# A two-attention transformer layer in fp32: how the scores and the weighing of the values go through TensorE

## Chip, cores and metric

One core of one Trainium2 chip. The metric is device time in microseconds of one execution. TensorE (PE) multiplies and transposes, VectorE (DVE) and ScalarE (ACT) read its results from PSUM, GpSimd (POOL) works on SBUF alone, SyncE (SP) issues the DMAs.

## The reference

32 sequences of 128 tokens, 512 features, 16 heads of 32. In fp32:

```python
ln_out = layernorm(hidden_states, ln1_s, ln1_b)
q, k, v = jnp.split(ln_out @ w_qkv + b_qkv, 3, axis=-1)
scores = jnp.einsum('bhqd,bhkd->bhqk', q, k) / jnp.sqrt(jnp.float32(HD))
scores = scores * mask - 10000.0 * (1.0 - mask)
probs = jax.nn.softmax(scores, axis=-1)
ctx = jnp.einsum('bhqk,bhkd->bhqd', probs, v)
x = hidden_states + ctx @ w_ao + b_ao
# the same once more, with queries from layernorm(x), keys and values from the encoder states
return x + gelu(layernorm(x) @ w1 + b1) @ w2 + b2
```

## The kernel before, in words

Matrix products take fp32 operands apart into a high and a low part, both of the faster type fp32r, and add up three products (low x high, high x low, high x high). Wherever a matrix is made that TensorE needs later, ScalarE makes the high part (a rounding copy) and VectorE the low part (what is left).

Attention works on groups `g` of two sequences (`b` 0 and 1): groups 0 to 15 self-attention, 16 to 31 cross-attention. A group has eight slots `n`; the loops run over groups, with a body of eight slots. In a slot each engine runs a written-out list of calls (the function `slot` of each engine, L629, L777, L928, L1075, and L436 for the DMA queue), and the order in it is fixed. Engines wait for each other by semaphores only. One slot is four heads (chunk `c`, 128 features) of one sequence: `c, b = divmod(n, 2)`.

What TensorE does for one group: the normalised x is transposed (`flip_x`, four 128x128 transposes; for cross groups the encoder rows too, `flip_enc`). `keys` and `queries` (`columns`, L519: 12 products of 256 columns) fill the bank `ps_c`; ScalarE and VectorE empty it into `k_r` and `q_r` before the next may start. `values` and `outputs` (`rows`, L530: two halves of six products of 512 columns) use the bank `ps_r`. For the scores of a slot, keys are placed block-diagonally in `k_bd` by DMA (`place_k`, four per chunk), so that one product of 512 columns gives four heads: three products (L492). VectorE multiplies by the mask (L837), POOL adds the mask's other part (L1046), VectorE takes the row maximum (L852). ScalarE negates it (L697) and takes four exponentials (L704), not normalised. TensorE transposes the four heads (L502), ScalarE and VectorE make an fp16 high and low part (L688, L843), and TensorE multiplies each with the values in three bf16 parts and a column of ones (`v_b`, L515: eight products of 97 columns). VectorE adds the three parts, inverts the sum and multiplies (L864, L866, L870) to give `ctx_t`, which is transposed when a sequence is complete (`flip_ctx`) and goes to `outputs`.

The softmax runs through the slots with a lag: scores of slot n, maximum and exponentials of n-1, transposes of n-2, values of n-3. Keys and queries of chunk c+1 are made in the slots of chunk c, so that each slot of TensorE has scores, transposes, a product with the values, and one or two of `keys`, `queries`, `values` and `outputs`. Layer norms of the next group (L900 to L926, `root` on POOL) lie between the slots' calls. The MLP follows when attention has ended; it shares only the weights' buffers and `mlp_xT` with it.

Lines that the prediction speaks of: L492 scores, L502 transposes, L515 values, L524 columns, L536 rows, L594 flips, L675 (`bias_products`, the only product of true fp32 operands), L688, L697, L704, L723 on ScalarE, L837, L852, L870, L885, L900, L915, L924 on VectorE, L1046 and L1072 on POOL.

Of the kernel before, what the change touches and what calls it, by code (L numbers as in the profile page):

```python
# [8 lines left out]
F32 = mybir.dt.float32  # L9
# [5 lines left out]
P = 128  # L15
# [5 lines left out]


LIFT = 15.0 * math.log(2.0)
VW = 3 * HD + 1
VPAD = VW + 1
# [33 lines left out]
def xattn_layer(nc, a, out):  # L59
# [22 lines left out]
    with ExitStack() as top:  # L82
# [17 lines left out]
        lift_t = sb("lift_t", [P, 1])  # L100
        s_const = sem("const_ready")
        CONSTANTS = 7
# [25 lines left out]
        k_bd = sb("k_bd", [P, 2, 2, GB, HQ * P], F32R)  # L128

        assert GB * HQ * 2 == KC * MB  # L130
        mlp_xT = k_bd[:].rearrange("p i h b t -> p (i h b t)").rearrange("p (h c t) -> p h c t", h=2, c=KC)
# [16 lines left out]
        def pieces(st, u, chunks=range(KC)):  # L148
# [7 lines left out]
            (-1, 4): pieces(SELF, WK), (-1, 5): pieces(SELF, WQ), (-1, 6): pieces(SELF, WV),  # L156
            (1, 0): pieces(SELF, WO),
            (NG - 1, 3): pieces(CROSS, WV, FRONT), (NG - 1, 4): pieces(CROSS, WK),
            (NG - 1, 5): pieces(CROSS, WQ), (NG - 1, 6): pieces(CROSS, WV, BACK),
            (NG + 1, 0): pieces(CROSS, WO),  # L160
# [71 lines left out]
        kbd_in = [sem(f"kbd_in{i}") for i in range(2)]  # L232
        names = ("sc_done pt_done pv_done k_done q_done v_done o_done xT_done encT_done cT_done exp_done pth_done "
                 "kh_done qh_done v1_done v2_done xTh_done encTh_done cTh_done masked mx_done nb_done ptl_done "
                 "kl_done ql_done vr_done v0_done y_copied xTl_done encTl_done cTl_done stats_done aggr_done "
                 "rstd_done xn_done centred eps_added sums_done ctx_done y_done biased v3_done mask_ready res_ready kbd_clear ones_ready")
        s = {name: sem(name) for name in names.split()}

        def attention(st):

# [20 lines left out]
            q_r = buf("q_r", [P, 2, 2, GB * P], F32R)  # L261
            k_r = buf("k_r", [P, 2, 2, GB * P], F32R)
            v_b = buf("v_b", [P, GB, NH, VPAD], BF16)
            v_rest = buf("v_rest", [P, GB, H])
# [3 lines left out]
            nb = buf("nb", [P, 2, HQ])  # L268
            pT = buf("pT", [P, 2, 2, HQ * P], F16)
            csum = buf("csum", [P, 2, HQ, HD])  # L270
            rcp = buf("rcp", [P, 2, HQ])
            ctx_t = buf("ctx_t", [P, GB, H])
# [19 lines left out]
            def leads(g):  # L292


                return isinstance(g, int) and g >= gN
# [27 lines left out]
            def run(engine, slot):  # L323


                for n in range(4, NS):
                    slot(-1, n, False, False, True)
# [1101 lines left out]
```

## Time and profile before

| what | value |
|---|---|
| device time, median of 3 | 2083.93 us (2080.98 to 2086.44) |
| profiled execution: span from first to last instruction | 2081.6 us |
| busy: PE, DVE, ACT, POOL | 94%, 67%, 52%, 42% |
| attention ends, MLP begins | about 1346 us |
| PE's mean granted clock | 0.993 of full |

The page gives no other time for the profiled execution than its span; it is 2.3 us below the median of the runs. In rows of the order of time, the first number is the start and the second the duration of the run of equal instructions; a bracket is the engine's idle time in front of it and what ended that. Durations overlap: the next instruction of an engine starts before the end of the one in front, so that the distance from start to start is the cost of an instruction in a queue.

### The profile page before, as it was taken

What the parts mean: (1) busy time and instruction counts of PE and PEld (TensorE: products, weight loads), DVE (VectorE), ACT (ScalarE), POOL (GpSimd) and SP (SyncE); (2) the same over time, 40 slices, a digit from 0 to 9 for tenths busy, and PEclk for the clock granted to TensorE, in tenths of its full rate; (3) what the DMA queues carried; (4) which work ended last, traced back from release to release, by engine and by line L of the source; (5) the groups of instructions that cost most, each with busy time, mean ns of one, the idle gap of its engine ahead of it and who ended that gap; (6) DMA issues with size and microseconds to landing.
All of it is one profiled execution on the core that took longest, in us unless ns stands there. A gap on an engine that the chain in (4) does not pass through costs nothing. (4 is left out here: it accounts for less than half of the span.)

```text
span 2081.6 us, 39412 instructions
## 1 busy us (share of the span) xinstructions
PE 1957.9 (94%) x12304; PEld 1657.1 (80%) x12304; DVE 1390.2 (67%) x2571; ACT 1072.6 (52%) x2562; POOL 884.1 (42%) x910
## 2 busy tenths in 40 slices
PE   5999999999998999999999999699999999999999
PEld 5788888888787778887887887588888888888887
DVE  6889889888888998899889888662322323232221
ACT  4666666667667666666676666443222222222222
POOL 5556556556557655555565555450201012020110
PEclk9999999999999999999999999899999999999999
DMA  6332222222223432332232224501010101101010
GB/s 172 94 91 70 65 77 68 66 72 74 61 73 88 106 97 73 86 93 72 77 96 71 73 83 104 165 28 51 11 55 5 60 12 48 50 10 54 6 41 21
DMA packets 144820, 141.51 MB, mean 68 GB/s; under 512 B 20736, under 2 KB 94464, under 8 KB 144768
## 3 DMA queue, kind: packets, MB, share of 16 engines
q1 hardware_dynamic: 144768, 140.85, 24.2%
q8 instruction: 28, 0.46, 0.1%
q14 instruction: 24, 0.20, 0.0%
HBM read 82.07 MB, written 25.17 MB: 52 GB/s over the span
## 5 line engine op out<-in xcount | busy, mean ns | idle before, releaser
L1046 POOL TENSOR_TENSOR a_t_s<-a_t_s,a_m_add 128x512 f32<-128x512 f32 x256 | 345.4, 1349 | 334.3 <-DVE a_t_s L837 334.1
L1315 DVE TENSOR_TENSOR m_g_r<-m_g_t,m_g_r 128x512 fp32r<-128x512 f32 x128 | 95.9, 750 | 476.1 <-ACT m_g_r L1294 476.0
L1223 PE MATMUL m_ps_h<-k_bd,wt 128*128 128x512 f32 x1536 | 378.7, 397 | 2.9 <-PEq L360 2.9
L1223 PEld LDWEIGHTS m_ps_h<-k_bd,wt 128*128 128x128 f32 x1536 | 289.2, 189 | 72.4 <-issue 3.3
L1237 PE MATMUL m_ps_y<-m_down_hi,m_g_r 128*128 128x512 f32 x1024 | 343.8, 396 | 0.1
L704 ACT ACTIVATE a_p_s<-a_t_s,a_nb 128x128 f32<-128x128 f32 x1024 | 328.3, 391 | 8.3
L524 PE MATMUL a_ps_c<-a_xT,wt 128*128 128x256 f32 x2304 | 318.2, 288 | 11.6 <-DVE a_xT L885 5.5
L524 PEld LDWEIGHTS a_ps_c<-a_xT,wt 128*128 128x128 f32 x2304 | 285.4, 191 | 25.3 <-issue 10.9
L1237 PEld LDWEIGHTS m_ps_y<-m_down_hi,m_g_r 128*128 128x128 f32 x1024 | 192.4, 188 | 45.1 <-issue 0.5
L1278 ACT ACTIVATE m_g_t<-m_ps_h,bias_cols 128x512 f32<-128x512 f32 x128 | 88.1, 688 | 270.9 <-PE m_ps_h L1223 270.7
L688 ACT CAST a_pT<-a_ps_t 128x512 f16<-128x512 f32 x256 | 150.0, 586 | 150.7 <-PE a_ps_t L502 150.4
L492 PE MATMUL a_ps_s<-k_bd,a_q_r 128*128 128x512 f32 x768 | 221.7, 397 | 0.0
L536 PE MATMUL a_ps_r<-wt,a_cT 128*128 128x512 f32 x768 | 209.2, 408 | 1.3 <-ACT a_y_t L752 1.3
L1376 POOL TENSOR_TENSOR m_rstd<-m_mv,eps_t 128x1 f32<-128x1 f32 x28 | 5.3, 189 | 478.6 <-DVE m_mv L1331 478.6
L843 DVE TENSOR_TENSOR a_pT<-a_ps_t,a_pT 128x512 f16<-128x512 f32 x256 | 174.3, 681 | 41.1 <-ACT a_pT L688 41.1
L1237 PE MATMUL m_ps_y<-wt,m_g_r 128*128 128x512 f32 x512 | 201.2, 393 | 0.0
L1294 ACT CAST m_g_r<-m_g_t 128x512 fp32r<-128x512 f32 x128 | 79.5, 621 | 236.0 <-PE m_ps_y L1237 234.6
L837 DVE TENSOR_TENSOR a_t_s<-a_ps_s,a_m_mul 128x512 f32<-128x512 f32 x256 | 174.3, 681 | 29.0 <-PE a_ps_s L492 27.8
L852 DVE TENSOR_REDUCE a_mx<-a_t_s 128x4 f32<-128x512 f32 x256 | 172.7, 675 | 2.5
L492 PEld LDWEIGHTS a_ps_s<-k_bd,a_q_r 128*128 128x128 f32 x768 | 140.1, 189 | 29.1 <-issue 1.0
L515 PE MATMUL a_ps_o<-a_v_b,a_pT 128*128 128x97 bf16 x2048 | 133.5, 207 | 29.3 <-POOL a_v_b L1052 14.9
L502 PEld LDWEIGHTS a_ps_t<-ident,a_p_s 128*128 128x128 f32 x1024 | 127.2, 140 | 42.3 <-ACT a_p_s L704 7.3
(85 smaller groups left out, 3210.9 us busy)
## 6 DMA issues: line engine op xcount, KB each, us to landing
k_bd<-a_k_r SPq DMA_DIRECT2D x512, 64.0 KB, 2.1
a_x_t<-in_x SPq DMA_DIRECT2D x32, 256.0 KB, 2.8
a_res_t<-in_x SPq DMA_DIRECT2D x32, 256.0 KB, 2.8
x_after_self<-a_y_t SPq DMA_DIRECT2D x32, 256.0 KB, 2.0
a_x_t<-x_after_self SPq DMA_DIRECT2D x32, 256.0 KB, 2.7
a_enc_t<-in_ctx SPq DMA_DIRECT2D x32, 256.0 KB, 2.9
raw_wt<-in_w SPq DMA_DIRECT2D x32, 256.0 KB, 4.7
a_res_t<-x_after_self SPq DMA_DIRECT2D x32, 256.0 KB, 3.9
```

The costliest lines, as they stand in the source:

```text
L492: last = nc.tensor.matmul(ps_s[n % 2][:], q_r[:, i, hq, b * P:(b + 1) * P], k_bd[:, i, hk, b], start=(x == 0), stop=(x == 2))
L515: last = nc.tensor.matmul(ps_o[:, j, 0:VW], pT[:, n % 2, h, j * P:(j + 1) * P], v_b[:, b, HQ * c + j, 0:VW], start=(h == HI), stop=(h == LO))
L524: last = nc.tensor.matmul(ps_c[:, 0:GB * P], weights(g, hw)[:, unit, kc, c * P:(c + 1) * P], xt[:, hx, kc], start=(k == 0), stop=(k == 3 * ...
L536: last = nc.tensor.matmul(ps_r[:], lhs(hx, kc), weights(g, hw)[:, unit, kc], start=(k == 0), stop=(k == 2 * n - 1))
L688: nc.scalar.copy(pT[:, n % 2, HI], ps_t[n % 2][:].rearrange("p j t -> p (j t)")).then_inc(s["pth_done"], 1)
L704: last = nc.scalar.activation(p_s[:, n % 2, j], t_s[:, n % 2, j], ACT.Exp, bias=nb[:, n % 2, j:j + 1])
L837: nc.vector.tensor_tensor(t_s[:, n % 2], ps_s[n % 2][:], m_mul[:, b].unsqueeze(1).to_broadcast([P, HQ, P]), ALU.mult).then_inc(s["masked"], 1)
L843: nc.vector.tensor_tensor(pT[:, n % 2, LO], ps_t[n % 2][:].rearrange("p j t -> p (j t)"), pT[:, n % 2, HI], ALU.subtract).then_inc(s["ptl_ ...
L852: nc.vector.tensor_reduce(mx[:, n % 2], t_s[:, n % 2], AX_X, ALU.max).then_inc(s["mx_done"], 1)
L1046: nc.gpsimd.tensor_tensor(t_s[:, n % 2], t_s[:, n % 2], m_add[:, b].unsqueeze(1).to_broadcast([P, HQ, P]), ALU.add).then_inc(s["biased"], 1)
L1223: last = nc.tensor.matmul(ps_h[j % 2][:], w1[hw][:, j // KC, kc, (j % KC) * P:(j % KC + 1) * P], xT[:, hx, kc], start=(k == 0), stop=(k == ...
L1237: last = nc.tensor.matmul(ps_y[b][:], g_r[:, j % 2, hg, b * P:(b + 1) * P], w2[hw][:, j // KC, j % KC], start=(j == 0 and x == 0), stop=(j ...
```

## The change

- Keys and queries stay in fp32 (`k_t`, `q_t`), copied out of `ps_c` by ScalarE alone. The scores of a whole sequence are made at once, for each head and chunk one fp32 product over the head's 32 rows, 128 columns; the four heads of a chunk lie in four 32-row strips and four PSUM banks. `k_bd` and its DMAs go.
- The order of heads in slots changes: `b, c = divmod(n, 4)`. All keys and queries of the next group are made in slots 4 to 7, values and outputs in slots 0 to 3.
- The exponentials give their sums too (`accum_out`). VectorE inverts the sums and normalises the probabilities, which TensorE transposes and ScalarE copies once, in fp32. Per head, fp32 values (32 columns) are the stationary operand and the transposed probabilities the moving one, so that the product comes out as a 32-partition strip of the transposed context, in `ps_o`; the context's flip goes.
- `ps_x` goes: flips use `ps_c`. There is one bank for `ps_t` instead of two.
- x is loaded two groups ahead; weight splits, stores and residual loads move to other slots.

```diff
-            ps_s = [ps(f"a_ps_s{i}", [P, HQ, P], F32, st) for i in range(2)]
-            ps_t = [ps(f"a_ps_t{i}", [P, HQ, P], F32, st) for i in range(2)]
-            ps_c = ps("a_ps_c", [P, H], F32, st)
+            ps_s = ps("a_ps_s", [P, HQ, KC, P], F32, st)
+            ps_t = ps("a_ps_t", [P, HQ, P], F32, st)
+            ps_c = ps("a_ps_c", [P, KC, P], F32, st)
             ps_r = ps("a_ps_r", [P, H], F32, st)
-            ps_o = ps("a_ps_o", [P, HQ, P], F32, st)
-            ps_x = ps("a_ps_x", [P, KC, P], F32, st)
+            ps_o = ps("a_ps_o", [P, KC, P], F32, st)
...
+                    def scores(g, b):
+                        pe.wait_ge(s["k_copied"], at((g + 1) * KC))
+                        pe.wait_ge(s["q_copied"], at((g + 1) * KC))
+                        if b > 0 or known(g, 1):
+                            pe.wait_ge(s["masked"], at((g * GB + b) * KC))
+                        cols = slice(b * P, (b + 1) * P)
+                        for c in range(KC):
+                            for j in range(HQ):
+                                r = slice(HD * j, HD * (j + 1))
+                                last = nc.tensor.matmul(ps_s[:, j, c], q_t[r, c, cols], k_t[r, c, cols],
+                                                        start=True, stop=True)
+                        last.then_inc(s["sc_done"], 1)
...
                     def transpose_probs(g, n):
+                        pe.wait_ge(s["normal"], at(slot_no(g, n)))
+                        if n >= 1 or known(g, 1):
+                            pe.wait_ge(s["pT_copied"], at(slot_no(*lag(g, n, 1))))
...
                     def weigh_values(g, n):
+                        b, c = divmod(n, KC)
+                        pe.wait_ge(s["pT_copied"], at(slot_no(g, n)))
...
                         for j in range(HQ):
+                            h = HQ * c + j
+                            last = nc.tensor.matmul(ps_o[HD * j:HD * (j + 1), c], v_t[:, b, HD * h:HD * (h + 1)],
+                                                    pT[:, n % 2, j], start=True, stop=True)
...
                     def keys(g, c):
                         if c > 0 or known(g, 1):
-                            pe.wait_ge(s["ql_done"], at(g * KC + c))
+                            pe.wait_ge(s["q_copied"], at(g * KC + c))
                     def queries(g, c):
-                        pe.wait_ge(s["kl_done"], at(g * KC + c + 1))
+                        pe.wait_ge(s["k_copied"], at(g * KC + c + 1))
...
                     def flip_enc(g, b):
                         pe.wait_ge(enc_in[b], at(16 * (g - NG + 1)))
+                        pe.wait_ge(s["xTl_done"], at(g * GB + b + 1))
                         flip(enc_t, b, "encT_done")
...
                     def slot(g, n, cur, prev, nxt):          # TensorE
+                        if n in (0, 3) and prev:
+                            outputs(g - 1, n // 3, 0, cur)
+                        if n in (1, 2) and cur:
+                            values(g, n - 1, 0)
+                        if n >= 4 and nxt:
+                            keys(g + 1, n - 4)
+                        if n in (0, 1):
+                            if n == 0 and prev:
+                                outputs(g - 1, 0, 1, cur)
+                            if n == 1 and cur:
+                                values(g, 0, 1)
+                        if cur if n >= 3 else prev:
+                            weigh_values(*lag(g, n, 3))
+                        if n == 2 and cur:
+                            values(g, 1, 1)
+                        if n == 3 and prev:
+                            outputs(g - 1, 1, 1, cur)
+                        if n >= 4 and nxt:
+                            queries(g + 1, n - 4)
                         if cur if n >= 2 else prev:
                             transpose_probs(*lag(g, n, 2))
...
+                        if n in (2, 3) and nxt:
+                            flip_x(g + 1, n - 2)
+                            if crosses(g + 1):
+                                flip_enc(g + 1, n - 2)
+                        if n == 3 and cur:
+                            scores(g, 1)
                         if n == 7 and nxt:
+                            scores(g + 1, 0)
...
                     def exponent(g, n):                      # ScalarE
                         act.wait_ge(s["mx_done"], at(slot_no(g, n)))
-                        nc.scalar.activation(nb[:, n % 2], mx[:, n % 2], ACT.Identity, bias=lift_t[:],
-                                             scale=-1.0).then_inc(s["nb_done"], 1)
...
                         for j in range(HQ):
                             last = nc.scalar.activation(p_s[:, n % 2, j], t_s[:, n % 2, j], ACT.Exp,
-                                                        bias=nb[:, n % 2, j:j + 1])
+                                                        bias=mx[:, n % 2, j:j + 1],
+                                                        accum_out=sums[:, n % 2, j:j + 1])
...
+                        if cur if n >= 3 else prev:
+                            copy_probs(*lag(g, n, 3))
                         if cur if n >= 1 else prev:
                             exponent(*lag(g, n, 1))
+                        if n >= 4 and nxt:
+                            copy_cols(g + 1, n - 4, WK, k_t, "k_done", "k_copied")
+                        if n == 2 and prev:
+                            high_context(g - 1, 1)
+                        if n == 6 and cur:
+                            high_context(g, 0)
                         if cur or prev:
                             split_weights(g, n)
+                        if n in (0, 3) and prev:
+                            output_row(g - 1, n // 3)
+                        if n in (1, 2) and cur:
+                            copy_values(g, n - 1)
+                        if n >= 4 and nxt:
+                            copy_cols(g + 1, n - 4, WQ, q_t, "q_done", "q_copied")
...
+                        if n in (2, 3) and nxt:
+                            flip_x(g + 1, n - 2)
...
+                    def invert_sums(g, n):                   # VectorE
+                        dve.wait_ge(s["exp_done"], at(slot_no(g, n)))
+                        nc.vector.reciprocal(rcp[:, n % 2], sums[:, n % 2]).then_inc(s["inverted"], 1)
+                    def normalise(g, n):
+                        dve.wait_ge(s["inverted"], at(slot_no(g, n)))
+                        nc.vector.tensor_tensor(p_s[:, n % 2], p_s[:, n % 2],
+                                                rcp[:, n % 2].unsqueeze(2).to_broadcast([P, HQ, P]),
+                                                ALU.mult).then_inc(s["normal"], 1)
...
+                        if n == 2 and ahead:
+                            norm(g + 1, 1)
                         if cur if n >= 1 else prev:
                             maxima(*lag(g, n, 1))
                         if cur:
                             mask_scores(g, n)
+                        if n == 0 and ahead:
+                            statistics(g + 1, 0)
+                            statistics(g + 1, 1)
                         if cur if n >= 2 else prev:
+                            invert_sums(*lag(g, n, 2))
...
                         if cur if n >= 2 else prev:
+                            normalise(*lag(g, n, 2))
...
+                            moments(g + 1, 0)
+                            moments(g + 1, 1)
+                        if n == 1 and ahead:
+                            centre(g + 1, 0)
+                            norm(g + 1, 0)
+                            centre(g + 1, 1)
+                        if n == 2 and prev:
+                            low_context(g - 1, 1)
+                        if n == 6 and cur:
+                            low_context(g, 0)
...
+                        if n in (2, 3) and nxt:
+                            flip_x(g + 1, n - 2)
+                            if crosses(g + 1):
+                                flip_enc(g + 1, n - 2)
```

## Rows read from the trace of the kernel before

**Rows 1.** The page: busy time, and the span in 40 slices (digits are tenths).
```profile
PE 1957.9 (94%) x12304; PEld 1657.1 (80%) x12304; DVE 1390.2 (67%) x2571; ACT 1072.6 (52%) x2562; POOL 884.1 (42%) x910
...
PE   5999999999998999999999999699999999999999
...
DVE  6889889888888998899889888662322323232221
```

**Rows 2.** Windows: stretch, its length, busy us (instructions) per engine, TensorE's clock, DMA.
```profile
401.30:440.60 39.30, 37.09 (x282) 32.56 (x281) 34.71 (x69) 26.14 (x69) 23.44 (x25) 1.00 0.27 70
...
1004.30:1045.00 40.70, 38.28 (x292) 33.32 (x290) 36.53 (x71) 27.12 (x71) 23.43 (x25) 1.00 0.30 81
1302.00:1346.00 44.00, 27.90 (x168) 22.02 (x166) 30.82 (x56) 19.04 (x46) 21.35 (x19) 0.81 0.46 150
1346.00:2081.00 735.00, 729.38 (x3184) 588.49 (x3184) 219.96 (x314) 198.21 (x313) 99.48 (x102) 1.00 0.10 35
```

**Rows 3.** TensorE's order of time: start, duration, line, tiles, count, idle time before.
```profile
410.36 0.63 PE L594 MATMUL a_ps_x<-ident,a_xn 128*128 128x128 f32 x4 [1.56 <-DVE a_xT L885]
...
415.61 1.64 PE L536 MATMUL a_ps_r<-wt,a_cT 128*128 128x512 f32 x6
417.09 1.53 PE L524 MATMUL a_ps_c<-a_xT,wt 128*128 128x256 f32 x12
418.45 0.86 PE L492 MATMUL a_ps_s<-k_bd,a_q_r 128*128 128x512 f32 x3
419.15 0.60 PE L502 MATMUL a_ps_t<-ident,a_p_s 128*128 128x128 f32 x4
419.59 0.52 PE L515 MATMUL a_ps_o<-a_v_b,a_pT 128*128 128x97 bf16 x8
419.93 1.63 PE L524 MATMUL a_ps_c<-a_xT,wt 128*128 128x256 f32 x12
421.39 1.54 PE L536 MATMUL a_ps_r<-wt,a_xT 128*128 128x512 f32 x6
...
648.94 0.63 PE L594 MATMUL a_ps_x<-ident,a_enc_t 128*128 128x128 f32 x4 [2.28 <-DVE a_encT L885]
```

**Rows 4.** TensorE's order of time where the true fp32 products run.
```profile
64.86 3.60 PE L675 MATMUL a_ps_x<-raw_wt,a_cv 128*128 128x512 f32 x8
```

**Rows 5.** ScalarE's order of time in one slot.
```profile
418.65 0.47 ACT L723 ACTIVATE a_q_r<-a_ps_c,bias_cols 128x256 fp32r<-128x256 f32 x1 [0.94 <-PE a_ps_c L524]
...
419.79 0.58 ACT L688 CAST a_pT<-a_ps_t 128x512 f16<-128x512 f32 x1 [0.19 <-PE a_ps_t L502]
420.27 0.30 ACT L697 ACTIVATE a_nb<-a_mx,lift_t 128x4 f32<-128x4 f32 x1
420.60 1.28 ACT L704 ACTIVATE a_p_s<-a_t_s,a_nb 128x128 f32<-128x128 f32 x4
```

**Rows 6.** VectorE's order of time, four of its instructions.
```profile
402.60 1.58 DVE L915 SCALAR_TENSOR_TENSOR a_xn<-a_x_t,a_mv,norm_row 128x512 f32<-128x512 f32 x1
404.10 0.74 DVE L924 SCALAR_TENSOR_TENSOR a_xn<-a_xn,a_rstd,norm_row 128x512 f32<-128x512 f32 x1
...
407.88 1.35 DVE L870 TENSOR_TENSOR a_ctx_t<-a_csum,a_rcp 128x128 f32<-128x128 f32 x1
...
410.73 0.67 DVE L837 TENSOR_TENSOR a_t_s<-a_ps_s,a_m_mul 128x512 f32<-128x512 f32 x1
```

**Rows 7.** POOL's order of time beside them.
```profile
407.81 1.26 POOL L1072 TENSOR_TENSOR a_res_t<-a_res_t,bias_row 128x512 f32<-128x512 f32 x1
411.48 1.29 POOL L1046 TENSOR_TENSOR a_t_s<-a_t_s,a_m_add 128x512 f32<-128x512 f32 x1 [2.41 <-DVE a_t_s L837]
```

**Rows 8.** TensorE's order of time: the first scores and the last.
```profile
29.88 0.86 PE L492 MATMUL a_ps_s<-k_bd,a_q_r 128*128 128x512 f32 x3
...
1313.27 0.86 PE L492 MATMUL a_ps_s<-k_bd,a_q_r 128*128 128x512 f32 x3
```

**Rows 9.** One line's instructions, 66 to 1300 us: durations in ns, minimum, median, maximum.
```profile
L870 DVE TENSOR_TENSOR a_ctx_t<-a_csum,a_rcp x243: 291/294/1360, 71.5 to 1296.3; 128x128 f32<-128x128 f32 x122
```

More of the change, by code:

```diff
@@ L20 @@
 MASKED = 10000.0
-LIFT = 15.0 * math.log(2.0)
-VW = 3 * HD + 1
-VPAD = VW + 1
 HI, LO = 0, 1
@@ L231, in xattn_layer @@
         stored = [sem(f"stored{b}") for b in range(GB)]
[L232 to L236, printed above, removed]
+        names = ("sc_done pt_done pv_done k_done q_done v_done o_done xT_done encT_done cT_done exp_done pT_copied "
+                 "k_copied q_copied v_copied xTh_done encTh_done cTh_done masked mx_done inverted normal "
+                 "y_copied xTl_done encTl_done cTl_done stats_done aggr_done "
+                 "rstd_done xn_done centred eps_added y_done biased mask_ready res_ready")
         s = {name: sem(name) for name in names.split()}
@@ L323, in run @@
             def run(engine, slot):
-                for n in range(4, NS):
+                for n in range(2, NS):
                     slot(-1, n, False, False, True)
@@ L331, in run @@
                     slot(1, n, True, True, True)
-                with engine.Fori(0, NG - 3) as i:
+                with engine.Fori(0, NG - 4) as i:
                     g = Looped(i, 1, 2)
@@ L342, in run @@
                         slot(g, n, True, True, True)
+                for n in range(NS):
+                    slot(gN - 2, n, True, True, True)
                 for n in range(NS):
@@ L875, in low_cols @@
-                    def low_cols(g, c, unit, dst_t, high, low):
-                        dve.wait_ge(s[high], at(g * KC + c + 1))
-                        i = c % 2
-                        nc.vector.scalar_tensor_tensor(
-                            out=dst_t[:, i, LO], in0=ps_c[:, 0:GB * P],
-                            scalar=bias_cols[:, crosses(g), KC * unit + c:KC * unit + c + 1], in1=dst_t[:, i, HI],
-                            op0=ALU.add, op1=ALU.subtract).then_inc(s[low], 1)
-                    def low_flip(hi_t, lo_t, high, count, low):
+                            dve.wait_ge(s["exp_done"], at(slot_no(*lag(g, n, 2))))
@@ L934, in slot @@
                             mask_scores(g, n)
-                        if n == 4 and ahead:
-                            norm(g + 1, 1)
+                        if n == 0 and ahead:
+                            statistics(g + 1, 0)
+                            statistics(g + 1, 1)
                         if cur if n >= 2 else prev:
-                            low_probs(*lag(g, n, 2))
-                        if n in (1, 2) and ahead:
-                            statistics(g + 1, n - 1)
-                        if n in (2, 3) and prev:
-                            flip_ctx(g - 1, n - 2)
@@ L971, in slot @@
+                        if not (cur or prev) and n >= 4:
+                            split_weights(g, n)
                         if n in (0, 1, 4, 5) and leads(g):
                             flip_x(g + n // 4, n % 4)
-                        if n in (1, 3) and ahead:
-                            centre(g + 1, n // 2)
-                        if n == 3 and ahead:
-                            norm(g + 1, 0)
                     def spread_value_bias(st):
```

415 lines of the change are left out of this document (119 added, 296 removed).

## The prediction, made before the change was run

> **What bounds the kernel now.** The busy table and the slices come first: TensorE is at nine tenths nearly everywhere, VectorE at eight to nine until the 25th slice, then it falls [rows 1]. So there are two stages: attention, 16 self and 16 cross groups of two sequences, until 1346 us [rows 2], then the MLP, 735 us with TensorE 99% busy [rows 2], which the change leaves alone. The windows by stage give one period: 39.3 us for a self group, 40.7 for a cross group, TensorE busy for 37.1 and 38.3 of them [rows 2]. TensorE's order of time shows a slot without waits (417.09 to 421.39 us): columns 1.36 to 1.46, rows 1.48, scores 0.70, transposes 0.44, values 0.34, start to start [rows 3]. TensorE's queue bounds attention, and its one long wait in a self group is the flip of x that waits for the one before it, 1.56 us [rows 3].
>
> **TensorE's work.** A true fp32 call is two instructions: the eight L675 instructions (four calls, 512 columns) take 3.60 us, 0.43 each, against 0.25 for a single-pass one (1.48 by six) [rows 3, 4]. A 128-column fp32 instruction takes 0.11 (transposes, 0.44 by four). Scores become 16 calls, 32 instructions, per sequence. Side by side in no way they cost 32 x 0.108 = 3.45 us; fed as fast as the values of before, eight in 0.34 us, 32 cost 1.36. I take 1.75: a call's two halves use the same 32 rows and run in turn (16 x 0.107), neighbours overlap. Values become 8 instructions per slot, 0.34 to 0.86; by the same argument 0.43. The context's flip (four transposes, 0.44) goes, twice per group. TensorE's sum is then 8 x 1.46 + 8 x 1.48 + 8 x 0.44 + 2 x 0.44 + 2 x 1.75 + 8 x 0.43 = 34.9 us per self group, less than the 37.1 of now: the question is only who makes it wait.
>
> The Trainium skill, "TensorEngine Tiling (Array Packing)", section Theoretical Speedup, gives up to 4x where a dimension is at most 32. By it scores would take 0.86, and the sum below would be some 28 us less. The same page, section Key Properties, says that a change of tiling mode drains the engine; no row here shows a switch, but a drain as long as the tail of the transposes (0.60 busy for 0.44 of pitch) at the four edges of scores would make it some 20 us more.
>
> **Slots 4 to 7: one loop through ScalarE.** There is one bank, ps_c, for the columns. Keys fill it, ScalarE copies it, queries may start (k_copied), ScalarE copies again, the next keys may start (q_copied). ScalarE's own order in the slot is copy_probs, the four exponentials, copy of keys, copy of queries; behind a late exponential stand both copies, and TensorE waits for them. Before, other TensorE work stood between the two fills of ps_c in every slot; now only the short values. The loop [rows 5]: copy_probs 0.49 (0.58 less the overlap of 0.09), exponentials E, key copy 0.46, semaphore 0.05, queries 1.45 plus 0.20 until ScalarE sees the end [rows 3], query copy 0.46 less 0.06: 3.05 + E, near enough. E is 1.19 now. The sums (accum_out) have no row. Free, E stays 1.19, below which it can't fall. As four further instructions like the smallest of ScalarE, L697 with 0.30 [rows 5], without overlap, E is 4 x (0.39 + 0.30) = 2.76. The nearest row is that instruction with the overlap of its neighbours: 4 x (0.30 + 0.21) = 2.04, which I take. Loop: 5.05 us (4.2 to 5.8), where a slot is 4.9 now on the mean.
>
> **Slots 0 to 3: a chain through VectorE.** VectorE loses low_probs, the context's reduction and product and low_cols; it gets a reciprocal (0.2) and normalise. That product is from SBUF, 128x512: 0.66 as L924 (0.74 less an overlap of 0.08), but such instructions wait for POOL: L870 took 1.35 instead of 0.29 beside POOL's 407.81 instruction, and centre (L915) 1.58 instead of 0.74 [rows 6, 7]. POOL starts add_bias 0.08 after the mask ends (411.40, 411.48), 1.29 long, so normalise behind the mask usually stands some 1.2. From the scores' end, VectorE does: slot 0, maximum and mask 1.2, two statistics 1.2 (priced as the mask), reciprocal and normalise 0.9, POOL 0.3, moments 0.2; slot 1, maximum, mask, reciprocal, normalise 2.1, centre, norm, centre 2.0, and 0 to 2.6 for POOL's two additions, of which I take 0.65; slot 2, norm 0.66, maximum and mask 1.2, POOL 1.37, normalise 0.66. With 0.2 to see the scores, the probabilities of slot 0 are normalised at 12.6. TensorE asks for them at 2 x (2.96 + 0.43 + 0.44) + 2.96 + 0.43 = 11.05, and waits. Then a chain: transposes 0.44, flip 0.44, 0.2, ScalarE 0.58, VectorE's low part 0.62, maximum 0.60, mask 0.67, POOL 1.37, normalise 0.70: 5.6, because the low part stands in front of the next maximum in VectorE's order. Then transposes and flip 0.88 and scores 1.75, which cover the wait of keys for the second flip (0.2 + 0.58 + 0.62). Slots 0 to 3: 12.6 + 5.6 + 0.88 + 1.75 = 20.8.
>
> **The sum.** Self group: 20.8 + 4 x 5.05 + 1.75 (scores of slot 7) = 42.75, +3.45. A cross group flips the encoder's rows too, through the same ps_c, directly behind x: twice 0.44 and a wait of 1.45 (0.25, 0.58, 0.62; 2.28 and 1.56 in like places now [rows 3]), 3.8 in all: 46.55, +5.85. The 31 periods but the last, 15.5 of each kind: 15.5 x 9.3 = +144. Edges: all keys and queries of group 0 now come ahead of the first scores (29.9 us now [rows 8]), some +7; the last group has no next columns and flips, and behind its last scores there are fewer steps than in the 33 us of now: together -15 (-30 to +10). The block-diagonal placements on SP's queue go; in the rows above TensorE waits for none of them, so they give nothing. POOL's lost value splits (1.1 each, four per group) shorten no wait but those counted. 2081.6 + 144 - 15 = 2211, and with the 2.3 us by which the median, 2083.9, is above this execution's span: **2213 us**.
>
> **Rivals.** (1) *ScalarE's loop stays as short as today.* Sums cost nothing (E = 1.19), and POOL lets normalise pass in slots 0 and 1 so that TensorE doesn't wait at 11.05. For it: L870's median is 0.29, so most of them met no POOL [rows 9]; before, ScalarE waits long per group for TensorE, busy 26.1 of 39.3 us [rows 2]. Against: POOL now follows the mask directly. Self 11.05 + 5.6 + 0.88 + 1.75 + 4 x 4.24 + 1.75 = 38.0, cross 41.8: 15.5 x (-1.3 + 1.1) - 15 = -18, **2066**: faster. It decides where the pair's gain of 15.5 periods crosses +15: each 0.1 of E is 0.8 per pair, so at E of 1.4 with the probabilities on time, and never with them at 12.6. (2) *The tiles run one after the other*: scores 3.45, values 0.86. The values hide under the loop and the waits; scores add 1.7 twice: 31 x 3.4 = +105, **2318**. For it: no row shows two TensorE instructions at once. (3) *All waits fall into gaps and TensorE's sum binds*: 34.9 and 35.8 (with two more flips), 15.5 x (-4.4 - 4.9) - 15 = -159, **1925**. Against: both loops are written-out orders around one bank. (4) *Sums at half my price*, E = 1.6: 15.5 x 5.8 - 15 = +75, **2159**; with E near 1.2 and late probabilities it comes near no change.
>
> **Chances.** Forecast and its neighbourhood (2165 to 2275) 0.42; (4), 2075 to 2165, 0.20, with 0.06 of it within 0.3%, about what a measurement here can tell from no change; (2) 0.19; (1) 0.14; (3) 0.05. Faster is (1) less a little, plus (3): 0.18. Same 0.06. Slower 0.76. The range reaches from 2060, just under (1)'s time, to (2)'s 2318.
>
> **What would show it.** Slots 4 to 7: ScalarE nearly without gaps but for queries, TensorE's columns waiting for ScalarE's copies in most of the 128 slots; the exponentials' group at 0.5 us per head. Slots 2 and 3: TensorE's transposes waiting for VectorE's normalise, whose mean is above 1.2 us. Cross groups over 3 us longer than self groups. TensorE's clock, full in the groups now [rows 2], should stay there; it was 0.81 where TensorE was busy 27.9 of 44 us [rows 2], and if the waits bring that on, all is later. Scores at 1.4 to 2 us per sequence; 3.4 makes (2) true. The forecast is wrong if keys and queries run back to back.

## The result and the profile after

The changed kernel takes 2261.74 us (median of 4 runs, 2259.72 to 2265.16) where the kernel before, on the same chip, takes 2084.84: a ratio of 1.0852, 95% interval 1.0837 to 1.0868. It is slower by 177 us; the forecast, 2213, had 129, and the range reached from 2060 to 2318. One execution of a kernel further down, bank and normalise first, took 3643.7 us, and its median leaves that one out.

The page of the changed kernel, span and slices, answers to [rows 1]:
```profile
span 2259.7 us, 39332 instructions
...
PE 1961.6 (87%) x13328; PEld 1546.0 (68%) x13328; DVE 1280.8 (57%) x1802; ACT 1030.6 (46%) x3202; POOL 780.0 (35%) x778
...
PE   6888888888887888788887878869999999999999
...
PEclk9999999999998999899999899979999999999999
```
TensorE falls from 94% to 87%, with nearly the same busy time (1961.6 and 1957.9 us) in a longer span, and no other engine is busier than before. The time went into waits, and into slower work where TensorE's granted clock fell (0.958 on the mean, 0.993 before).

The windows of the changed kernel answer to [rows 2]: a self group, a cross group, the last groups' end, the MLP.
```profile
434.69:477.22 42.53, 35.23 (x317) 27.47 (x313) 31.31 (x44) 24.62 (x90) 20.37 (x20) 1.00 0.13 40
1110.04:1157.82 47.78, 38.51 (x322) 29.89 (x321) 32.68 (x46) 25.91 (x90) 20.36 (x20) 0.93 0.14 47
1480.00:1523.88 43.88, 27.12 (x180) 18.36 (x179) 27.03 (x42) 21.17 (x70) 17.59 (x16) 0.71 0.36 129
1523.88:2259.00 735.12, 730.32 (x3184) 589.25 (x3184) 219.46 (x314) 198.07 (x313) 99.45 (x102) 1.00 0.10 34
```
The MLP is as long as it was, 735 us. A self group went from 39.30 to 42.53, a cross group from 40.70 to 47.78: 15.5 x (3.23 + 7.08) = 160 us of the 177. The other 17 are at the edges. In the self group TensorE is busy for less than before (35.23 us, 37.09 before); in the cross group, at a granted clock of 0.93, it isn't (38.51, 38.28 before).

TensorE's order of time in that self group (columns as in [rows 3]): slots 1 to 3, the scores, then slots 4 to 7.
```profile
443.80 0.42 PE L471 MATMUL a_ps_o<-a_pT,a_v_t 128*32 128x128 f32 x8
444.16 1.66 PE L492 MATMUL a_ps_r<-wt,a_xT 128*128 128x512 f32 x6
448.92 0.66 PE L459 MATMUL a_ps_t<-ident,a_p_s 128*128 128x128 f32 x4 [3.10 <-DVE a_p_s L757]
...
454.63 0.66 PE L459 MATMUL a_ps_t<-ident,a_p_s 128*128 128x128 f32 x4 [1.28 <-DVE a_p_s L757]
455.13 0.60 PE L545 MATMUL a_ps_c<-ident,a_xn 128*128 128x128 f32 x4
455.66 1.17 PE L450 MATMUL a_ps_s<-qk 32*128 32x128 f32 x32
457.13 1.65 PE L480 MATMUL a_ps_c<-a_xT,wt 128*128 128x256 f32 x12 [0.30 <-DVE a_xT L763]
458.71 0.43 PE L471 MATMUL a_ps_o<-a_pT,a_v_t 128*32 128x128 f32 x8
459.76 1.64 PE L480 MATMUL a_ps_c<-a_xT,wt 128*128 128x256 f32 x12 [0.63 <-ACT qk L641]
...
476.12 1.17 PE L450 MATMUL a_ps_s<-qk 32*128 32x128 f32 x32 [0.31 <-ACT qk L641]
477.22 3.06 PE L492 MATMUL a_ps_r<-wt,a_cT 128*128 128x512 f32 x12
```
Both waits of the forecast are there: 3.10 and 1.28 us for VectorE's normalise (L757) in slots 2 and 3, then in each of slots 4 to 7 a wait for ScalarE's copy (L641). The scores of one sequence take 1.10 us from start to start (476.12 to 477.22).

What VectorE and POOL did ahead of that 3.10, in order of time:
```profile
439.51 1.56 POOL L930 TENSOR_TENSOR a_res_t<-a_res_t,bias_row 128x512 f32<-128x512 f32 x1
439.82 1.79 DVE L793 SCALAR_TENSOR_TENSOR a_xn<-a_x_t,a_mv,norm_row 128x512 f32<-128x512 f32 x1
441.03 1.72 POOL L915 TENSOR_TENSOR a_t_s<-a_t_s,a_m_add 128x512 f32<-128x512 f32 x1
441.65 1.65 DVE L802 SCALAR_TENSOR_TENSOR a_xn<-a_xn,a_rstd,norm_row 128x512 f32<-128x512 f32 x1
442.71 1.73 POOL L923 TENSOR_TENSOR a_y_t<-a_y_t,a_res_t 128x512 f32<-128x512 f32 x1
443.22 1.77 DVE L793 SCALAR_TENSOR_TENSOR a_xn<-a_x_t,a_mv,norm_row 128x512 f32<-128x512 f32 x1
...
447.05 1.26 POOL L915 TENSOR_TENSOR a_t_s<-a_t_s,a_m_add 128x512 f32<-128x512 f32 x1 [2.61 <-DVE a_t_s L736]
447.09 1.77 DVE L757 TENSOR_TENSOR a_p_s<-a_p_s,a_rcp 128x512 f32<-128x512 f32 x1
```
The two engines take turns: three POOL additions, and three VectorE instructions of 1.65 to 1.79 that take 0.75 or less alone. Then the mask sets off POOL's addition at 447.05, normalise starts 0.04 later and takes 1.77 instead of the 0.69 that it takes elsewhere. Over the kernel its 256 instances mean 1418 ns.

### The profile page after: what moved, and what is told of

It reads as the page before. It is cut to its first block and busy times, and to the rows that moved or that the text cites. A ratio compares the mean times of both kernels' runs of the same rounds, so it can differ in the third digit from the quotient of the medians.

```text
span 2259.7 us, 39332 instructions
## 1 busy us (share of the span) xinstructions
PE 1961.6 (87%) x13328; PEld 1546.0 (68%) x13328; DVE 1280.8 (57%) x1802; ACT 1030.6 (46%) x3202; POOL 780.0 (35%) x778
## 5 line engine op out<-in xcount | busy, mean ns | idle before, releaser
L629 ACT ACTIVATE a_p_s<-a_t_s,a_mx 128x128 f32<-128x128 f32 x1024 | 398.6, 392 | 172.9 <-DVE a_mx L746 172.8
L480 PE MATMUL a_ps_c<-a_xT,wt 128*128 128x256 f32 x2304 | 327.6, 293 | 76.8 <-ACT qk L641 64.4
L1075 PE MATMUL m_ps_h<-mlp_xT,wt 128*128 128x512 f32 x1536 | 379.6, 398 | 1.8 <-PEq L338 1.8
L757 DVE TENSOR_TENSOR a_p_s<-a_p_s,a_rcp 128x512 f32<-128x512 f32 x256 | 362.9, 1418 | 11.0
L1075 PEld LDWEIGHTS m_ps_h<-mlp_xT,wt 128*128 128x128 f32 x1536 | 289.9, 189 | 71.3 <-issue 2.0
L459 PE MATMUL a_ps_t<-ident,a_p_s 128*128 128x128 f32 x1024 | 165.9, 286 | 120.9 <-DVE a_p_s L757 120.8
L492 PE MATMUL a_ps_r<-wt,a_cT 128*128 128x512 f32 x768 | 244.5, 469 | 1.4 <-DVE a_cT L763 1.4
L459 PEld LDWEIGHTS a_ps_t<-ident,a_p_s 128*128 128x128 f32 x1024 | 116.9, 144 | 157.5 <-DVE a_p_s L757 145.4
L641 ACT ACTIVATE qk<-a_ps_c,bias_cols 128x256 f32<-128x256 f32 x256 | 118.9, 464 | 221.2 <-PE a_ps_c L480 221.2
L492 PEld LDWEIGHTS a_ps_r<-wt,a_cT 128*128 128x128 f32 x768 | 166.0, 228 | 48.4 <-issue 9.5
L629 ACT ACTIVATION_READ_ACCUMULATOR a_p_s<-a_t_s,a_mx 128x1 f32 x1024 | 193.2, 189 | 0.0
```

Source lines behind the costliest of these rows:

```text
L459: last = nc.tensor.transpose(ps_t[:, j], p_s[:, n % 2, j], ident[:])
L480: last = nc.tensor.matmul(ps_c[:, 0:GB], weights(g, hw)[:, unit, kc, c * P:(c + 1) * P], xt[:, hx, kc], start=(k == 0), stop=(k == 3 * KC ...
L492: last = nc.tensor.matmul(ps_r[:], lhs(hx, kc), weights(g, hw)[:, unit, kc], start=(k == 0), stop=(k == 2 * n - 1))
L629: last = nc.scalar.activation(p_s[:, n % 2, j], t_s[:, n % 2, j], ACT.Exp, bias=mx[:, n % 2, j:j + 1], accum_out=sums[:, n % 2, j:j + 1])
L641: nc.scalar.activation(dst_t[:, c], ps_c[:, 0:GB].rearrange("p b t -> p (b t)"), ACT.Identity, bias=bias_cols[:, crosses(g), KC * unit + c ...
L757: nc.vector.tensor_tensor(p_s[:, n % 2], p_s[:, n % 2], rcp[:, n % 2].unsqueeze(2).to_broadcast([P, HQ, P]), ALU.mult).then_inc(s["normal" ...
```

## The experiments

All times are medians; the ratio is to runs of the kernel before on the same chip. The changed kernel stands at 1.0852.

| kernel: the changed one, with | us | ratio (95%) |
|---|---|---|
| no sums | 2238.3 | 1.0751 (1.0733 to 1.0769) |
| keys copied first | 2237.9 | 1.0744 (1.0725 to 1.0763) |
| queries in another bank | 2143.1 | 1.0299 (1.0282 to 1.0316) |
| one strip after another | 2370.0 | 1.1385 (1.1357 to 1.1413) |
| POOL's additions moved | 2185.1 | 1.0505 (1.0466 to 1.0543) |
| normalise first | 2093.9 | 1.0049 (1.0023 to 1.0076) |
| encoder's flip later | 2266.1 | 1.0872 (1.0830 to 1.0914) |
| bank + POOL + flip | 2073.0 | 0.9947 (0.9931 to 0.9964) |
| bank + normalise first | 1981.9 | 0.9517 (0.9498 to 0.9536) |
| bank + normalise first + flip | 1976.4 | 0.9492 (0.9476 to 0.9508) |
| bank + normalise first + POOL | 1980.0 | 0.9498 (0.9479 to 0.9517) |
| bank + normalise first, no sums | 1970.1 | 0.9458 (0.9442 to 0.9474) |

**The loop through one bank (slots 4 to 7).** *No sums:*
```diff
-    bias=mx[:, n % 2, j:j + 1], accum_out=sums[:, n % 2, j:j + 1])
+    bias=mx[:, n % 2, j:j + 1])
...
-nc.vector.reciprocal(rcp[:, n % 2], sums[:, n % 2])
+nc.vector.reciprocal(rcp[:, n % 2], mx[:, n % 2])
```


> Leaves out: the exponentials write no sums (no accum_out), and the reciprocal reads the maxima instead, so the division is by the wrong number; every wait and every other instruction stay. In the changed kernel an exponential with its sum has a pitch of 0.385 us, four per slot 1.54, where the kernel before has 1.19. Theory A (slots 4 to 7 go round one bank by way of ScalarE, so every 0.1 us of ScalarE in a slot is 31 x 4 x 0.1 = 12 us): the pitch falls to 0.30, 0.34 us per slot, 43 us in all: 2261.7 - 43 = 2219. Rival B (the waits for ScalarE's copies are only where the slack shows; the softmax chain of VectorE and POOL paces the slots): less than 10 us, 2252 or more.

*Keys copied first:*
```diff
+if n >= 4 and nxt:
+    copy_cols(g + 1, n - 4, WK, k_t, "k_done", "k_copied")
 if cur if n >= 1 else prev:
     exponent(*lag(g, n, 1))
-if n >= 4 and nxt:
-    copy_cols(g + 1, n - 4, WK, k_t, "k_done", "k_copied")
```


> Same work; in slots 4 to 7 ScalarE copies the keys before the four exponentials of the slot instead of behind them. Theory A (the loop through ScalarE is what TensorE waits for): the exponentials then run beside the queries, and the loop is keys 1.4, 0.2 to see the end, copy 0.45, 0.05, queries 1.45, 0.2, copy 0.45, 0.05 = 4.25 instead of the measured 4.75 per slot: 31 x 4 x 0.5 = 62 us less, 2200. Rival B (VectorE and POOL pace the slots): the exponentials come 0.45 us later, reciprocal and normalise with them, and the time stays at 2262 or rises a little, up to 2275.

*Queries in another bank (ps_r):*
```diff
-last = nc.tensor.matmul(ps_c[:, 0:GB],
+last = nc.tensor.matmul(ps_r[:, 0:GB * P].rearrange("p (b t) -> p b t", b=GB) if unit == WQ else ps_c[:, 0:GB],
...
 def keys(g, c):
-    pe.wait_ge(s["q_copied"], at(g * KC + c))
+    pe.wait_ge(s["k_copied"], at(g * KC + c))
...
 def queries(g, c):
-    pe.wait_ge(s["k_copied"], at(g * KC + c + 1))
+    if c > 0:
+        pe.wait_ge(s["q_copied"], at(g * KC + c))
+    elif known(g, 2):
+        pe.wait_ge(s["y_copied"], at((g - 1) * GB))
+    elif known(g, 1):
+        pe.wait_ge(s["v_copied"], at(g * GB))
```


> The queries of slots 4 to 7 go through the bank ps_r, which is idle there (values and outputs use it in slots 0 to 3 only); keys keep ps_c. So keys and queries no longer wait for one another's copies; same work. Theory A (that loop was all that TensorE waited for in slots 4 to 7): a slot falls from 4.75 to TensorE's own 1.4 + 0.36 + 1.45 + 0.44 = 3.7 us (ScalarE's sum is about 3.1): 31 x 4 x 1.05 = 130 us less, 2132. Rival B (VectorE and POOL come next: maximum 0.6, mask 0.67, POOL 1.4, reciprocal and normalise 0.9 to 2.0, in series 3.6 to 4.7 per slot): at 4.3 a slot 56 us less, 2206. If both are wrong and the copies never set the pace: 2262.

Without sums, and with keys first, the kernel gained 23 and 24 us; theory A had 43 and 62, rival B none. Both edits shorten TensorE's wait for the copies: the columns from x show 64.4 us of it in the changed kernel, 32.3 without sums, 33.7 with keys first, and those from the encoder 0.4, 0.3 and 7.6. The trace without sums is of a run of 2218.2 (granted clock 0.960), which meets theory A's 2219; the other four took 2235.8 to 2239.7 (0.949 to 0.953), and no trace shows where, so what the sums are worth lies between 23 and 43. The loop doesn't get shorter with either edit than a floor of the single bank, which I had not set apart. TensorE's order with keys first shows it, queries, keys and queries again:
```profile
457.63 1.66 PE L480 MATMUL a_ps_c<-a_xT,wt 128*128 128x256 f32 x12 [0.21 <-ACT qk L641]
...
459.86 1.68 PE L480 MATMUL a_ps_c<-a_xT,wt 128*128 128x256 f32 x12
...
462.10 1.66 PE L480 MATMUL a_ps_c<-a_xT,wt 128*128 128x256 f32 x12 [0.21 <-ACT qk L641]
```
Fill, see, copy and see again take 2.23 us, twice per slot: 4.47, where the changed kernel has 4.65 in the like slot (459.76 to 464.41). Without sums the like distance is 4.42 (447.98 to 452.40 there). So these edits were worth two tenths a slot, and the bank the rest: with queries in ps_r the line of the columns shows no wait for a copy any more, and the time falls by 119 us, where theory A had 130. Of the 119, 13 are at the start, which theory A didn't count, because the same loop ran there too. The first columns of the changed kernel, and then of the kernel with ps_r and normalise first:
```profile
19.18 2.93 PE L480 MATMUL a_ps_c<-a_xT,wt 128*128 128x256 f32 x12 [2.50 <-DVE a_xT L763]
...
43.69 2.93 PE L480 MATMUL a_ps_c<-a_xT,wt 128*128 128x256 f32 x12 [0.56 <-ACT qk L641]
47.27 2.09 PE L450 MATMUL a_ps_s<-qk 32*128 32x128 f32 x32 [0.66 <-ACT qk L641]
```
```profile
20.78 2.93 PE L481 MATMUL a_ps_c<-a_xT,wt 128*128 128x256 f32 x12 [2.42 <-DVE a_xT L770]
23.51 1.61 PE L481 MATMUL a_ps_r<-a_xT,wt 128*128 128x256 f32 x12
24.95 1.52 PE L481 MATMUL a_ps_c<-a_xT,wt 128*128 128x256 f32 x12
...
34.02 1.17 PE L450 MATMUL a_ps_s<-qk 32*128 32x128 f32 x32 [0.74 <-ACT qk L648]
```
Back to back, seven of the eight blocks take about half the time, and the first scores come 13 us earlier.

**The tiles.** *One strip after another:*
```diff
-for c in range(KC):
-    for j in range(HQ):
+for j in range(HQ):
+    for c in range(KC):
         r = slice(HD * j, HD * (j + 1))
```


> Same work; the 16 calls of a sequence's scores are issued with the strip of 32 rows in the outer loop, so that four calls in a row use the same strip, where before neighbours used different ones. Theory A (the 1.10 us for 32 instructions come from neighbours on different strips running side by side): one after the other they take 32 x 0.107 = 3.4 us, up to +2.3 us per sequence; in slot 7 all of it counts, in slot 3 part of it lies beside the wait for the flip: 31 x 2.3 to 31 x 4.6 = +71 to +143, 2333 to 2405. Rival (an instruction of 32 rows costs 0.034 us whichever strip its neighbour uses): 2262.

Slower by 108 us, inside theory A. TensorE's order there, scores and what follows:
```profile
440.94 2.82 PE L450 MATMUL a_ps_s<-qk 32*128 32x128 f32 x32
443.68 1.68 PE L480 MATMUL a_ps_c<-a_xT,wt 128*128 128x256 f32 x12
```
2.74 us instead of 1.10: 0.086 per instruction on one strip, 0.034 when neighbours are on different strips. So neighbours on different strips overlap; a strip alone is also somewhat cheaper than the 0.107 that I took from 128 rows. The edit puts neighbours into one PSUM bank as well, and no run parts the strip from the bank. Against the bank as the cause speak the values: eight in a row, all into the bank of `ps_o` (on four strips of its partitions), start every 0.045 us (443.80 to 444.16).

**The late probabilities (slots 0 to 3).** *POOL's additions moved:*
```diff
-if n in (1, 4) and prev: output_row(g - 1, n // 4)
-if n == 0 and prev:      residual(g - 1, 1)
+if n in (3, 4) and prev: output_row(g - 1, n - 3)
+if n == 7 and cur:       residual(g, 1)
...
-if n in (2, 5) and prev: store(g - 1, n // 5)
+if n in (4, 5) and prev: store(g - 1, n - 4)
```


> Same work; POOL's residual addition of slot 0 goes to slot 7 of the group before and its output row of slot 1 to slot 3 (the store two slots later), so that in slots 0 and 1 POOL has only the two mask additions and no addition stands between the mask and the normalise. Theory A (the probabilities of slot 0 are late because three POOL additions and four VectorE instructions take turns in slot 1, 439.5 to 445.8 us): the normalise comes 2.5 us earlier, 31 x 2.5 = 78 us less, 2184; TensorE's clock, 0.958 on the mean, comes back towards the 0.993 of before. Rival C (POOL and VectorE hinder each other wherever the additions stand, or VectorE's own order of centre, norm, centre ahead of the probabilities is what is late): within 12 us, 2250 to 2270.

*Normalise first:*
```diff
 maxima(*lag(g, n, 1))
-mask_scores(g, n)
 invert_sums(*lag(g, n, 2))
 normalise(*lag(g, n, 2))
+mask_scores(g, n)
```
With it, `moments` and VectorE's wait for the statistics, and POOL's `root`, go from slot 0 to slot 1; `root` stands ahead of the slot's `add_bias` there.


> Same work; VectorE does reciprocal and normalise ahead of the mask of the slot instead of behind it (the norm's two small moments, and POOL's roots of them, go from slot 0 to slot 1). Theory A (normalise takes 1.42 us on the mean instead of 0.69 because the mask in front of it sets off POOL's addition, and TensorE waits for it in slots 2 and 3): the mean falls to about 0.7, and in slots 2 and 3 the probabilities come 1 to 2 us earlier each: 31 x 2 to 31 x 4 = 62 to 124 us less, 2140 to 2200. Rival C (the pair of VectorE and POOL is a series anyway: the mask, POOL's addition and the next maximum come later by what normalise gains): 2250 to 2275, with a mean of 0.7 all the same.

POOL's move gave 77 us for 78 expected, and the clock of the profiled run went from 0.958 to 0.977. Normalise stayed at 1421 ns; what became shorter is the layer norm ahead of it (L793 1220 ns on the mean instead of 1698, L802 777 instead of 1203). TensorE's first wait fell from 3.10 to 1.19:
```profile
459.05 0.66 PE L459 MATMUL a_ps_t<-ident,a_p_s 128*128 128x128 f32 x4 [1.19 <-DVE a_p_s L757]
```
The second stayed, 1.26 for 1.28. Normalise first gives 168 us (six runs, 2087.8 to 2102.5), more than theory A's 62 to 124. The two lines of normalise and of the transposes behind it in that kernel:
```profile
L757 DVE TENSOR_TENSOR a_p_s<-a_p_s,a_rcp 128x512 f32<-128x512 f32 x256 | 199.1, 778 | 8.7
...
L459 PE MATMUL a_ps_t<-ident,a_p_s 128*128 128x128 f32 x1024 | 159.2, 278 | 9.5 <-DVE a_p_s L757 9.4
```
The mean is 778 ns instead of 1418, and the transposes wait 9.4 us for normalise instead of 120.8. A self group takes 38.27 us. But the edit does two things. With the roots ahead of it, POOL's addition in slot 1 comes later, and three of the layer norm's four instructions are through before it. VectorE and POOL in slots 1 and 2:
```profile
440.42 0.73 DVE L793 SCALAR_TENSOR_TENSOR a_xn<-a_x_t,a_mv,norm_row 128x512 f32<-128x512 f32 x1
...
441.86 0.75 DVE L793 SCALAR_TENSOR_TENSOR a_xn<-a_x_t,a_mv,norm_row 128x512 f32<-128x512 f32 x1
442.32 1.43 POOL L912 TENSOR_TENSOR a_t_s<-a_t_s,a_m_add 128x512 f32<-128x512 f32 x1
...
445.01 0.97 DVE L757 TENSOR_TENSOR a_p_s<-a_p_s,a_rcp 128x512 f32<-128x512 f32 x1
```
The two instructions of L793 took 1.79 and 1.77 in the changed kernel. Counted from the end of the scores, the normalise for which TensorE waited 3.10 us ends at 14.2 in the changed kernel (434.69 to 448.86), at 12.3 with POOL's additions moved (446.74 to 459.00), at 10.3 here (435.65 to 445.98). So the late probabilities have two causes of about equal size: POOL's additions beside the layer norm, and normalise behind the mask. The table parts them: POOL's move alone gave 77 us, and between two kernels that both have it (and the bank), 2073.0 and 1980.0, normalise first gives 93 us, which lies inside theory A's range; these two differ by the flip besides. What part of either is TensorE's clock, 0.992 here, no run separates. Rival C falls: the mask and the addition do come later, but nothing on TensorE waits for them yet.

**The encoder's flip.**
```diff
 outputs(g - 1, n // 3, 0, cur)
+if n == 3 and nxt and crosses(g + 1): flip_enc(g + 1, 0)     # was in slot 2
```


> Same work; in cross groups TensorE's first flip of the encoder's rows goes from the end of slot 2 to slot 3, behind the first half of the output rows, so that it stands at a place where x has been copied out of the bank already. Theory A (that wait, 1.5 to 1.65 us in each cross group of the changed kernel, is on the path): 15.5 cross groups x 1.55 = 24 us less, 2238, and cross groups keep 45 to 46 us instead of 47.8. Rival (the second flip, the values' chain or the next columns then wait as much longer): 2255 to 2265.

No gain: 2266.1 (2255.0 to 2273.9), near the rival's 2255 to 2265. TensorE's wait ahead of the flip fell from 49.8 to 24.4 us, its wait for ScalarE's copy of the probabilities rose from 5.5 to 24.1, and its wait for normalise from 120.8 to 140.6. I moved the flip on TensorE but not the copy on ScalarE, and the copy of the probabilities stands behind that one.

**Together.** *Bank, POOL and flip:*

> Three edits together, same work: queries through ps_r in slots 4 to 7, POOL's residual and output row out of slots 0 and 1, the encoder's flip behind the output rows. Theory A (the loop of slots 4 to 7 and the late probabilities of slots 0 to 3 are two waits in different stretches, so their prices add): 2262 - 119 - 77 - 24 = 2042, faster than the kernel before, and TensorE's clock at 0.98 or more. Rival (with the loop gone, VectorE and POOL bind over the whole group, so the second edit gives less than half of its own 77): 2090 or more, still slower than before.

2073.0 us, 0.5% below the kernel before, and between theory A's 2042 and the rival's 2090. POOL's move and the flip together gave 70 us on top of the bank's 119. The flip alone gave nothing; without its 24, theory A has 2066, so the bank and POOL's move add but for 7 us.

*Bank and normalise first:*

> Two edits together, same work: queries through ps_r in slots 4 to 7, and reciprocal and normalise ahead of the mask on VectorE. With normalise first alone TensorE waits nowhere in slots 0 to 3 of a self group, and in slots 4 to 7 only for ScalarE's copies, 4.67 us a slot. Theory A (the two waits are all that the change lost in its groups): a slot falls to TensorE's own 3.75, 31 x 4 x 0.92 = 114 us less than 2094, so 1980, some 5% faster than the kernel before. Rival (the softmax chain over VectorE, POOL and ScalarE, maximum 0.6, reciprocal and normalise 0.9, mask 0.6, addition 1.3 and their semaphores, then paces the slots at 4.0 or more): 2010 to 2050.

1981.9 us for 1980 expected. The window of a self group, and the first scores of a cross group and of the next:
```profile
385.21:420.01 34.80, 33.92 (x316) 27.54 (x312) 24.73 (x44) 24.83 (x90) 20.46 (x20) 1.00 0.16 49
```
```profile
996.21 1.17 PE L450 MATMUL a_ps_s<-qk 32*128 32x128 f32 x32 [0.31 <-ACT qk L648]
...
1034.97 1.17 PE L450 MATMUL a_ps_s<-qk 32*128 32x128 f32 x32 [0.31 <-ACT qk L648]
```
The self group takes 34.80, close to the sum of TensorE's work that the prediction had, 34.9; with the scores as measured that sum is 33.6, so about a microsecond of waits is left. The cross group takes 38.76. So with the bank and the two orders (what VectorE does ahead of the mask, and what POOL does ahead of its addition) the change is worth 5%; without them it cost 8.5%, a difference of 280 us.

*The three probes on top of it:*

> As the run with queries in ps_r and normalise first, and the encoder's first flip moved behind the first half of the output rows. By itself that move gave nothing, because TensorE waited for late probabilities at the same place instead. Theory A: with the probabilities on time the wait of 1.65 us in each cross group now goes, 15.5 x 1.65 = 25 us less than that run, some 1955. Rival (it is taken up again by another wait): within 6 us of that run.

> As the run with queries in ps_r and normalise first, and POOL's residual and output row out of slots 0 and 1. Theory A (POOL's place mattered only because normalise stood behind the mask; with normalise first no TensorE instruction waits for the pair of VectorE and POOL): within 8 us of that run, where it was worth 77 us in the changed kernel. Rival (POOL in slot 1 still delays the chain of norm and maximum): 20 to 77 us less.

> As the run with queries in ps_r and normalise first, but the exponentials write no sums and the reciprocal reads the maxima (the division is by the wrong number). Theory A (the sums cost only by way of the loop through ps_c, which is gone): within 6 us of that run, where they were worth 23 us in the changed kernel. Rival (ScalarE is still on the path of the probabilities): 20 to 43 us less.

The flip gave 5.5 us, not 25, within the rival's 6: at 1976.4 the fastest version that does the whole work, but by intervals that overlap. Its lines show why, values first, then the flip:
```profile
L471 PE MATMUL a_ps_o<-a_pT,a_v_t 128*32 128x128 f32 x2048 | 109.7, 286 | 26.1 <-ACT a_pT L628 26.1
...
L551 PE MATMUL a_ps_c<-ident,a_enc_t 128*128 128x128 f32 x128 | 20.0, 279 | 23.9 <-DVE a_xT L772 23.9
```
Without the move these waits are 7.1 and 50.8: 27 us less for the flip, 19 more for the values. POOL's move, worth 77 us before, is worth 2 on top of normalise first. That is theory A's number, but its reason is only half of it: the same edit had also taken POOL's additions off most of the layer norm. Leaving out the sums still gives 12 us, more than A's 6 and less than the rival's 20. In the profiles, 3.4 us of it is the outputs' wait for the context (5.1 to 1.7), 1.3 the flip's wait for the norm; where the rest is, I can't say.

## Why the prediction was right or wrong, step by step

- **Direction and mechanism: right.** The two waits forecast, one bank through ScalarE and normalise behind POOL, are more than the whole loss of 177 us. Taking away the first gives back 119, the second 168, both 280. The forecast had POOL's hold on VectorE at two places, beside the layer norm and behind the mask, and the runs show both; the first it had too small.
- **Self group, 42.75 forecast, 42.53 measured, with three errors that cancel, which is luck.** Slots 0 to 3 took 22.4 until the next columns (434.69 to 457.13), not 20.8; slots 4 to 7 took 4.75 each (457.13 to 476.12), not 5.05; the last scores 1.10, not 1.75.
- **The exponentials' sums, E = 2.04, mis-sized.** Their order on ScalarE, one head and the next:
```profile
462.75 0.39 ACT L629 ACTIVATE a_p_s<-a_t_s,a_mx 128x128 f32<-128x128 f32 x1
463.04 0.19 ACT L629 ACTIVATION_READ_ACCUMULATOR a_p_s<-a_t_s,a_mx 128x1 f32 x1
463.14 0.39 ACT L629 ACTIVATE a_p_s<-a_t_s,a_mx 128x128 f32<-128x128 f32 x1
```
  The added instruction takes 0.19, not 0.30, and the next head follows 0.39 behind the last (0.385 on the mean): E is 1.54. Rival (4), at 1.6, had the price right and 2159 wrong, since other terms were late. And rival (1) made E decide: the floor of one bank, 4.42 to 4.47, says that no price of E would have kept the loop at 4.24.
- **Normalised at 12.6: it was 14.2** behind the end of the scores (434.69 to 448.92). TensorE asked at 11.1, as forecast. I counted 0.65 us for two POOL additions beside the norm; there were three, and each pushed a VectorE instruction by a microsecond. The chain after it, 5.6, measured 5.71. I priced the order of normalise behind the mask as given, and never asked what the other order would do.
- **Cross group, +5.85: measured +7.08.** The waits at the encoder's flip were 1.65 and 1.49, for 1.45. Over the self group it takes 5.25 more, not 3.8. Behind the waits for normalise and for the flip TensorE is slow, and two products that take 1.64 and 1.67 us in the self group take:
```profile
1149.43 2.91 PE L492 MATMUL a_ps_r<-wt,a_cT 128*128 128x512 f32 x6
...
1152.85 2.05 PE L492 MATMUL a_ps_r<-wt,a_cT 128*128 128x512 f32 x6
```
  The window's granted clock was 0.93, where the prediction had it stay full and named the risk without a number. That this is the whole rest isn't shown, but with bank and normalise first, where the clock of a cross group is 1.00 (998.00 to 1036.07), it takes 3.96 more than a self group (38.76 and 34.80), near the forecast.
- **Edges, -15 (-30 to +10): +17, outside.** The first scores came 17.4 us later ([rows 8]: 29.88, now 47.27), where I had +7: eight blocks of columns at 3.5 each, of which I had not seen that they run at half speed and go round the one bank. From the last scores to the MLP it takes 38.1 us (1485.79 to 1523.88), more than the 33 of before, with waits of 0.6 to 2.3 for normalise and a granted clock of 0.71. This term, 32 us, and the cross group, 15.5 x 1.2 = 19, are nearly all that the forecast was short by, 49.
- **Rival (2), tiles in turn: wrong,** by 1.10 us and by the run on one strip. My 1.75 stood between; the estimate from the Trainium skill's up to fourfold ("TensorEngine Tiling (Array Packing)", Theoretical Speedup) was 0.86. Measured, 0.107 to 0.034 is 3.1 times, and strip against strip 2.5. The stop at a change of tiling, priced at 20 us, hardly shows: from the flip to the scores (455.13 to 455.66) it is 0.53, where four transposes take 0.44 without one.
- **Rival (3), TensorE's sum binds, 1925:** not in this kernel, but with the bank and the orders mended it came to 1982. Of the 57 us of difference, 46 are the cross group, 38.76 where I had 35.8 without the flip's waits (15.5 of them); the rest is mostly at the edges.

## What to carry to other kernels

When a change lets one bank serve two users in turn, price the whole round trip (fill, see, copy, see), not the copier's other work: cheaper work elsewhere can't go below it, and an idle bank in that stretch was the remedy here. Where VectorE and POOL work on the same softmax, look at what each VectorE instruction sets off on POOL: put what TensorE waits for ahead of it, keep POOL's additions off the VectorE work in front of that, and try the two one by one, since an edit that moves one can move the other. And when an instruction is moved on one engine, move its partner in the order of the engine that serves it.

## What the runs showed of the hardware that was not expected

- **POOL's addition holds up VectorE for one whole instruction, but only some instructions.** Normalise and the norm (both tensors in SBUF) take 1.65 to 1.79 us beside POOL for 0.69 to 0.75 alone. The maximum doesn't slow down; POOL and VectorE in order of time, with normalise first:
```profile
443.71 1.73 POOL L920 TENSOR_TENSOR a_y_t<-a_y_t,a_res_t 128x512 f32<-128x512 f32 x1
444.22 0.67 DVE L746 TENSOR_REDUCE a_mx<-a_t_s 128x4 f32<-128x512 f32 x1
```
  The Trainium skill ("SBUF — State Buffer", Who interferes with whom) says so: a VectorE instruction with two SBUF inputs contends with a GpSimd instruction that reads SBUF, the shared port pair is an exclusive lock, and a reduction never contends. The trace agrees with all three: normalise ends 0.55 us behind the end of POOL's addition (448.86, 448.31), and the maximum above takes 0.67 beside one.
- **TensorE ran at half speed for 28 us at the start, although the profile gives this window a granted clock of 1.00** (19.0 to 47.2). Blocks of columns took 2.93 us there with a pause of 0.56 behind most of them; the same blocks take 1.52 in the kernel with ps_r and normalise first. By these durations it is TensorE's lower level, 1.2 GHz against 2.4, which the granted clock doesn't show here. With ps_r the blocks are fast behind the first one, where there is no pause. In the kernel before, the third block is fast, behind two of 2.90 and pauses of 1.18 and 1.09:
```profile
27.02 1.65 PE L524 MATMUL a_ps_c<-a_xT,wt 128*128 128x256 f32 x12 [1.09 <-DVE a_q_r L878]
```
  So a pause alone doesn't decide; what does is left open.
